# A mixture-of-experts kernel: two expert weight loads move behind the first gathers, and TensorE gets 28 spare products

## The reference

```python
x = x + layernorm(attention(layernorm(x)))
x = x + layernorm(ffn(layernorm(x)))
```

```python
scores = softmax(x @ gate_w.T); topk_w, topk_idx = top_k(scores, 6)
...
buf[e, slot] = x of the first 64 tokens that chose expert e
d = (silu(buf @ w_gate[e]) * (buf @ w_up[e])) @ w_down[e]
y[token] = sum of topk_w * d over the token's experts that kept it
y = y + (silu(x @ sh_gate.T) * (x @ sh_up.T)) @ sh_down.T
```

## Time and profile before

| quantity | value |
|---|---|
| median of 3 runs | 1391.33 us (1388.62 to 1393.0) |
| profiled execution, device time | 1390.42 us |
| its span in the trace | 1387.4 us |
| PE busy | 1307.1 us (94% of the span) |
| DVE, ACT, POOL busy | 1109.4, 854.4, 793.6 us |
| bytes moved by DMA | 96.48 MB |

### The profile page before, as it was taken

One profiled execution on the slowest core, in us unless ns is written; L12 is line 12 of the kernel. 1 busy time (PEld: TensorE's weight loads), 2 busy tenths in 40 slices (PEclk: granted clock), 3 DMA queues, 4 the chain that ended last, 5 costly groups with the idle time before them and its releaser, 6 DMA issues.

```text
span 1387.4 us, 26788 instructions
## 1 busy us (share of the span) xinstructions
PE 1307.1 (94%) x8603; PEld 1144.5 (82%) x8603; DVE 1109.4 (80%) x3652; ACT 854.4 (62%) x2322; POOL 793.6 (57%) x1054
## 2 busy tenths in 40 slices
PE   7999999999999999999999999999999999798850
PEld 5898999999999999999999999999999988654420
DVE  7778787889788987998788978897889888654438
ACT  6677666666666666666566666666666665543324
POOL 5666565556555655556555656565556554746544
PEclk9999999999999999999999999999999999899975
DMA  9200000100010001000100001000100017999986
GB/s 294 67 1 16 1 17 9 43 16 17 2 43 24 17 1 43 24 1 17 43 24 1 16 19 32 16 17 9 36 24 17 1 35 219 270 264 289 273 256 268
DMA packets 50506, 96.48 MB, mean 70 GB/s; under 512 B 4705, under 2 KB 36930, under 8 KB 50370
## 3 DMA queue, kind: packets, MB, share of 16 engines
q1 hardware_dynamic: 44226, 85.33, 19.2%
q0 software_dynamic: 6144, 9.44, 3.3%
HBM read 68.27 MB, written 26.49 MB: 68 GB/s over the span
## 4 chain that ended last, share of the span: by engine, by line
PE 84%; DVE 5%; POOL 4%; DMA 3%; issue 3%; ACT 1%; POOLq 0%; DVEq 0%
PE bank_t L716 18%; PE bank_s L716 17%; PE bank_o L716 16%; PE bank_y L716 13%; PE bank_f L716 8%; PE bank_t L802 4%; PE bank_s L802 4%; POOL ffn_sums L2166 2%; PE bank_f L802 2%; DMA ffn_sums<-dsum,idx_s 2%; POOL xg L2153 1%; DVE fstat L1927 1%; DVE fa L1922 1%; DVE fa L1947 1%; DMA stage<-in_wq 0%
## 5 line engine op out<-in xcount | busy, mean ns | idle before, releaser
L1995 POOL TENSOR_TENSOR prob<-prob,rinv 128x512 f32<-128x512 f32 (+3 forms) x512 | 362.2, 725 | 250.6 <-DVE rinv L1534 250.2
L1130 ACT ACTIVATE prob<-prob,negmax 128x512 f32<-128x512 f32 (+3 forms) x512 | 283.2, 555 | 19.7 <-DVE negmax L1521 13.7
L1982 POOL TENSOR_TENSOR q_l<-q_sum,q_h 128x128 fp32r<-128x128 f32 x254 | 182.7, 740 | 107.7 <-ACT q_h L1110 104.9
L716 PE MATMUL bank_y<-wo_h,o_h 128*128 128x256 f32 x508 | 145.6, 287 | 0.6 <-DVE o_l L1548 0.6
L716 PE MATMUL bank_y<-wo_l,o_h 128*128 128x256 f32 x508 | 141.8, 279 | 0.0
L716 PE MATMUL bank_y<-wo_h,o_l 128*128 128x256 f32 x508 | 141.7, 279 | 0.0
L1143 ACT ACTIVATE pt_h<-bank_t 128x256 fp32r<-128x256 f32 (+3 forms) x208 | 89.7, 431 | 80.6 <-PE bank_t L802 73.1
L1143 ACT ACTIVATE pt_h<-bank_s 128x512 fp32r<-128x512 f32 (+3 forms) x203 | 88.0, 434 | 79.4 <-PE bank_s L802 74.0
L716 PE MATMUL bank_o<-pt_h,v_h 128*128 128x256 f32 x380 | 135.0, 355 | 0.7 <-DVE o_l L1548 0.7
L716 PE MATMUL bank_o<-pt_l,v_h 128*128 128x256 f32 x380 | 135.2, 356 | 0.0
L716 PE MATMUL bank_o<-pt_h,v_l 128*128 128x256 f32 x380 | 134.6, 354 | 0.0
(11 more groups left out here) (475 smaller groups left out, 4062.9 us busy)
## 6 DMA issues: line engine op xcount, KB each, us to landing
w_gu<-in_w_in SPq DMA_DIRECT2D x32, 704.0 KB
w_dn<-in_w_out SPq DMA_DIRECT2D x32, 320.0 KB
xio<-in_x SPq DMA_DIRECT2D x16, 512.0 KB, 4.6
token_table<-rows SPq DMA_DIRECT2D x8, 640.0 KB, 3.7
ffn_sums<-keys SPq DMA_DIRECT2D x4, 1024.0 KB
x_rows<-xio SPq DMA_DIRECT2D x8, 512.0 KB, 2.9
ffn_sums<-ytr SPq DMA_DIRECT2D x16, 256.0 KB, 2.5
fx<-x_rows SPq DMA_DIRECT2D x8, 512.0 KB
```

What stands on the lines that cost most here:

```text
L716: return pe.matmul(o, l, r, start=start, stop=stop, skip_group_check=True)
L1130: act.activation(p_, p_, ACT.Exp, bias=negmax[:, r, i:i + 1], scale=-1.0, accum_out=rsum[:, r, i:i + 1]).then_inc(exp_made, 1)
L1982: pool.tensor_tensor(l_[:, cols], sum_of(step)[:, cols], plain(h_)[:, cols], ALU.subtract).then_inc(pos_low, 1)
L1995: pool.tensor_tensor(p_, p_, rinv[:, r, i:i + 1].to_broadcast([P, (i + 1) * P]), ALU.mult).then_inc(prob_made, 1)
```

## The change

`GATHERS_FIRST` = 2 and `WARM_AGAIN` = 28 are new. SP issues pairs 10 and 11 no longer among the stores but behind all of them, just ahead of pair 12, and only after `dma_g[1]` has reached 16, that is when the second gather has landed. TensorE gets 28 products of `sg_h` and `su_h` into bank y0 behind `shared_down(LAST, 0)`. Nothing reads their result.

```diff
+        GATHERS_FIRST, WARM_AGAIN = 2, 28
...
             store_rows(LAST)
-            load_pair(NW - 2)
             store_ffn(L1, 1)
             store_x2(LAST)
             store_ffn(L1, 0)
             sp.wait_ge(tok_made, 1)
             sp.dma_start(firsts_dram.rearrange("o (j c) -> (o j) c", c=CAP), tok2[0:NE:2, 0:CAP]
                          ).then_inc(dma_firsts, 16)
-            load_pair(NW - 1)
             sp.wait_ge(dma_firsts, 16)
...
             store_ffn(LAST, 1)
             store_ffn(LAST, 0)
 
-            for j in range(NW, NP):
+            sp.wait_ge(dma_g[GATHERS_FIRST - 1], 16)
+            for j in range(NW - 2, NP):
                 load_pair(j)
...
             shared_down(LAST, 0)
 
+
+            pe.wait_ge(use("gu", L1, 0, 0)[2], 1)
+            for n in range(WARM_AGAIN):
+                mm(bank["y0"][:, 0:E], sg_h[:, 0, 0:P], su_h[:, 0, 0:E], start=True, stop=True)
```

## The result

| | before | after |
|---|---|---|
| median of 12 runs each, side by side | 1388.49 us (1384.91 to 1393.0) | 1391.28 us (1390.54 to 1395.33) |
| ratio, with its 95% interval | | 1.0027 (1.0016 to 1.0038) |
| profiled execution: device time, span, mean clock | 1390.42, 1387.4, 0.975 | 1390.75, 1388.9, 0.974 |

The change makes the kernel slower by 0.27%, 3.7 us (2.2 to 5.3). (The ratio goes by all executions and not by the two medians; these are 2.8 us apart, the two means 3.7.) I had forecast 0.8 us faster. The absolute time, 1391.28, lies close to my 1390.5, but only because the three runs I started from had a median of 1391.33; with more runs the kernel before is at 1388.5. Read as a difference, the forecast has the wrong sign. The change is within the 0.3% that I had called "the same", though the interval leaves zero out.

The account below looks back on a forecast made before the run. It took full DMA engines (1220 to 1331 us) and GpSimd's scatter chain as the bound. A 1.6 us head start, partly cancelled by 1.7 us of DMA debt, gave -0.8: 1391.33 - 0.8 = 1390.5 us, range 1386.7 to 1394.2.

Parts of the forecast that it names:

- Gathers 0 and 1 earlier: Start of the expert stage: gather 0 lands 3.0 to 4.9 us after issue, a gain of 1.2 to 3.1 us.
- The 28 products: Ahead of the first transposes: products end at 1210.9, first transpose 1.1 us later (bounds -0.4 and +2.8).
- Pairs 0 and 1 at full clock: First two experts' products 2.4 us shorter and their transposes 0.3 us shorter, together -2.7 us.
- The debt of the loads: Loads of pairs 10 and 11 put off: at 1220 the DMA engines have done 1.7 us less work.
- Gathers 2 to 7: These share the DMA engines with the moved loads; costed at nothing, with cover 0.4 us thin.
- What reaches the end: Scatter chain to the end: 1.6 us head start less 1.5 us for the debt; between -1.6 and -0.1, taken as -0.8.
- C: Clock at half through all 28 products: 1391.4 us, or 1394.1 if also low for the first pairs; chance 0.12.
- A: Head start comes through whole, experts start 3.1 us earlier: 1388.2 us, down to 1386.5; chance 0.24.
- B: Delayed loads hit gather 2 and scatters 0 to 3, making the kernel slower: 1397.0 us; chance 0.12.

Follow-up runs that it names:

- e9: The change itself, unaltered, timed once more against the kernel before: ratio 1.0026, +3.6 us.
- e18: The kernel before with the 28 products alone, both loads at their old places, second comparison: ratio 1.0009, +1.2 us.
- e3: The change without SP's wait for the second gather, against the kernel before: ratio 1.0019, +2.6 us.
- e7: The kernel before with 12 products in each of two TensorE gaps between 1198 and 1204 us, no load moved: ratio 0.9994, -0.8 us.
- e5: The kernel before with 84 products at the place of the change's 28, no load moved: ratio 1.0053, +7.4 us.
- e1: Loads of pairs 10 and 11 moved and waiting as in the change, no added products, against the kernel before: ratio 1.0008, +1.1 us.
- e16: The two moved loads with their wait and no products, second comparison against the kernel before: ratio 1.0007, +1.0 us.
- e2: The kernel before with the 28 products alone, both loads at their old places, first comparison: ratio 1.0019, +2.6 us.
- e11: Pairs 10 and 11 moved with the wait, 12 products in each of two earlier gaps, none behind, against the kernel before: ratio 1.0025, +3.5 us.
- e13: Pairs 9, 10 and 11 moved, 12 products in each of two earlier gaps, against the kernel before: ratio 1.0041, +5.7 us.
- e4: Only pair 11 moved behind the second gather, no added products, against the kernel before: ratio 1.0000, 0 us.

## Why the prediction was wrong

1. **Gathers 0 and 1 earlier: right.** Gather 0 was used 4.16 us after its issue, inside 3.0 to 4.9. In the twelve traces with pair 11 moved this is 3.2 to 4.3 us, in the other eight 5.2 to 7.3.
2. **The 28 products: by TensorE's records as forecast.** They end at 1210.6 with a low clock of 3.4 us, and the first transpose starts at 1210.48, 0.7 us later than before where I had 1.1:

```profile
1210.48 0.64 PE L1039 MATMUL bank_y<-ident,xg 128*128 128x128 f32 x4
```

3. **Pairs 0 and 1 at full clock, -2.7: the step that failed.** From the first transposes to scatter 0 the kernel after takes 12.9 us against 11.6 before: 1.2 us more, not 2.7 less. ScalarE had the turned rows only at 1213.28 (e9, e18 and e3: 1214.52, 1213.50, 1213.63), 2.2 us after their recorded end, so the products of pairs 0 and 1 started 2.8 us late. They took 3.84 us in place of 4.88 and not 2.5, since the clock fell again at 1215.0. The term itself was also too large: full clock all the way is worth 1.9 to 2.3 us there (e7, e5), and I had taken the one trace, with the clock at half for 10.2 us, for the rule, where the second has 3.4. Steps 2 and 3 together were to be -1.6 us; at scatter 0 the change is at +2 to +3, and the products alone cost +1.9 in the side-by-side times. Where the 2.2 us come from stays open.
4. **The debt of the loads: near in size, its effect not shown.** I had 1.7 us less work done at 1220. From 1190 to 1220 before and after are:

```profile
1190.00:1220.00 30.00, 22.63 (x144) 16.82 (x142) 17.13 (x48) 13.29 (x39) 17.36 (x21) 0.83 0.78 233
```

```profile
1190.00:1220.00 30.00, 23.21 (x158) 19.55 (x159) 16.40 (x45) 11.85 (x34) 17.34 (x21) 0.89 0.73 223
```

That is 1.5 us of DMA work less by the share and 0.3 MB or 1.0 us by the bytes. My sum had left out the stretch from 1204 to 1208.2, where the share fell from 1.03 to 0.57, and had taken the hole behind it as closed (0.91). The loads alone cost +1.0 (-0.3 to 2.4), which does not leave zero out.
5. **Gathers 2 to 7: nothing, right.** No wait of TensorE for a gather stands in the chain after. The gathers' landings are not recorded in that trace, so their latency stays unread.
6. **What reaches the end: not settled.** I netted a head start against the debt, at a rate of about a half. There was no head start to net. A long delay of the start is passed on in large part (e5: scatter 0 6.6 us late, and +7.4 in the time); for the small ones here scatter 0 and the time do not go together closely enough to give a rate. The parts alone add up within their intervals: +1.9 for the products and +1.0 for the loads are +2.9, and +3.7 (2.4 to 4.9) was measured over two comparisons.

Of the rivals, C came nearest in number only: in its worse form, half speed through the products and nothing won back, it gave +2.8 us. Its mechanism is not what the record of the clock shows, which is back at 1.0 at 1208.17 in the kernel after, some 9 products into the block. What it had right is that nothing was won back. A did not come about: the gathers were earlier, but TensorE was behind its own products. Without products the head start was lost as well: in e1 and e16 the first rows were there 3.2 us after the issue of gather 0, and scatter 0 came 17.7 and 19.6 us after it, no sooner than before by more than 0.1 us. B's first scatters were not seen to cost time; their landings are missing from the trace after.

**What stays open.** The pause: what TensorE does in it, and whether it is there without a profile. Half speed through all 28 products and four transposes (about 7 us from 1206.3) would give 1213.3 in the kernel after and fits e3, e9 and e18 within half a microsecond, but it misses e2 by 1 us, leaves the pauses without products unexplained, and e5's 84 products ran at the full clock. In e2 and e18 the transposes started only 0.9 and 0.7 us after VectorE first used gather 0's rows (1209.60 and 1209.99), so the length of the block alone does not make 1.9 us. So the +1.9 of the products is measured, and its split between their own length, the pause and the clock is not. Nor is it settled why two loads with gap products gave +3.5, +0.4 and -1.1.

## What to carry to other kernels

A load that is put off makes a gather land sooner (3.2 to 4.3 us in place of 5.2 to 7.3 here), but that is worth something only if it is what the next stage waits for and if the stage behind it can use the lead; here it was lost again with and without products. Price against it the bytes that have not moved when a stretch with full DMA engines begins, as a risk and not as a fixed sum. Spare products that keep TensorE busy did best in idle time ahead of the fall of the clock (-2.1 us); behind the last real work 8 cost nothing, 28 cost 1.9 and 84 cost 7.4. A forecast that rests on where the clock stands in one trace needs a second trace of the same kernel first, and so does a debt read from one trace: those of one kernel moved 256 and 231 GB/s in the same 30 us.

## What the runs showed of the hardware

- TensorE's recorded ends and the time at which ScalarE takes the result differ by 0.9 to 3.6 us once, up to a time between 1213 and 1216.2, in fourteen of fifteen traces with missing semaphore updates and in none of the five without. Elsewhere they differ by some 0.02 us (e5: 1218.88 and 1218.90).
- The clock's fall near 1205 is not fixed for a kernel: the two traces of the kernel before have it at half for 10.2 us and for 3.4 us. The Trainium skill ("TensorE: Matmul & The Clock Gate", Part 1, What's actually happening) says that the number of slow products at the start of a kernel varies between runs of it; these two traces show the like in its middle.
- With full DMA engines the rate still differs between executions: from 1220 to 1331 it is 299 GB/s in e11 and 283 in e13, at shares of 1.02 and 1.04.
- The time from scatter 0 to scatter 31 goes with the clock in part. In e3 and e4, where it did not fall between them, it is 115.9 and 115.8 us; in e1 and e13, with three and four falls, 123.3 and 128.1. But e18 without a fall takes 118.0 and e9 with three 118.7. The side-by-side times of one kernel spread by 5 to 11 us; what makes them differ was not tested by itself.
